# A gated two-layer Flamingo block on one core: nine barrier-ended stages merged into three regions, the local feed-forward begun inside the local attention's last steps, and one gelu moved ahead of norms

## The chip, the cores and the metric

One core of a Trainium2 chip runs the whole program. Its engines are PE (matrix multiply; PEld is its weight load), DVE (vector), ACT (activation functions), POOL (general purpose) and SP, which here only issues DMAs. The metric is the device time of one execution in microseconds (us); shorter is better. One execution was also taken by the hardware profiler; its trace is what is read below.

## The reference, cut to what matters

Four sub-blocks, each with a residual gate `tanh(g)`, on x of shape 4 x 512 x 128, all in float32 except the last.

```python
x = x + tanh(g_xattn[0]) * L0_xattn(layernorm(x), ctx)      # 16 heads over 77 keys, then layernorm, gelu FFN 128-512-128, layernorm
x = x + tanh(g_ffn[0])   * L0_ffn(layernorm(x))             # two layers, below
x = x + tanh(g_xattn[1]) * L1_xattn(layernorm(x), ctx, fside)  # 8 heads, scores gated by fside
x = x + tanh(g_ffn[1])   * L1_ffn(layernorm(x))             # one 128 x 128 product with fp8 rounding

def layer(x):                       # L0_ffn, DEPTH = 2
    q, k, v = split(shift_token(x) @ wqkv)          # 8 heads of 64
    q, k = rotary(l2norm(q) * qs, l2norm(k) * ks)
    x = x + local_attention(q, k, v) @ wo           # windows of 64, each sees itself and the one before
    h = layernorm(shift_token(x))                   # shift_token delays half of the columns by one token
    a, g = split(h @ w1 + b1)
    return x + (a * gelu(g)) @ w2 + b2
```

## The kernel before, in words

The 2048 tokens are 16 tiles of 128 (n or m = 0 to 15), four to a batch element u. x, y and base hold one row of 128 numbers per token and stay in SBUF throughout. Everything is written out by hand for each engine: an engine runs its own list in order and waits on semaphores.

There are nine stages: input and first queries; attention A (16 heads over the context); AF, the feed-forward behind it; local attention and local feed-forward of layer 0; the same two of layer 1; attention C; and the fp8 product. Each is a `stage(...)` block, which allocates its semaphores, lets each engine run its list, and ends in a barrier of all engines (L180), a clear of the stage's semaphores by POOL and a second barrier (L183).

```python
with nc.Block() as block:
    yield block, sems
nums = [s.num for s in sems]
nc.all_engine_barrier(sems_to_clear=range(min(nums), max(nums) + 1))
```

AF (L611 to L771) works per batch element u: statistics on DVE (`dve_stats`, L193 to L203), a reciprocal root on POOL (`pool_rstd`, L209), norms shared by DVE (L220) and ACT (L217), transposes on PE (L701), four hidden products (L709) with gelu on ACT (L754), `project(u)` on PE (L717, 32 matmuls), `add_ffn(u)` on DVE (L632), a second norm with the residual, `add_x(u)` (L640, L645), and a third norm that writes y, the input of layer 0. ACT's list ends in gelu(2), norm(0, y), gelu(3), norm(1, y), norm(2, y), norm(3, y).

Local attention (L789 to L1107) is a software pipeline over n = 0 to 21. At its start PE transposes y (L812), ACT copies the transposes into ht (L971, L972), and the first products are keys (L821), queries (L824) and values (L940). DVE forms the rotary products (L1030, L1033). In the last steps only the rear of the pipeline runs. For tile m these are: `values(m)` on PE (L865, L866) at step m + 4; division on DVE into `on` (L1080, L1084), called on(m) below; transposes of `on` on PE (L931) and their copy on ACT (L1011) at step m + 5; the output projection r(m) on PE (L893) and the residual addition y(m) on DVE (L1056) at step m + 6. values(m) waits for y(m - 2), since both use the same PSUM bank.

Local feed-forward (L1109 to L1266) works per u: PE shifts half the columns by one token with two matmuls (L1154, L1156), DVE takes statistics (L195, L196, L200, L203), POOL the root (L209), DVE and ACT write the two halves of the norm (L220, L217), PE transposes (L1125), ACT copies (L1183), PE makes three pairs of gate and value products (L1135, L1137), ACT the gelu (L1192), DVE the product with the value (L1240), and PE projects (L1148). `finish(u)` on DVE (L1247) adds the result to `base`, which POOL has made from y and a bias row (L1215).

Attention C (L1270 to L1478) starts with `entry(u)` on DVE (L1293), which adds the gated y to x. The last stage (L1480 on) ends in four output DMAs.

## Time and profile before

| what | us |
|---|---|
| median of the runs, lowest to highest | 763.54 (762.81 to 764.01) |
| the profiled execution's own time | 767.54 |
| its span from first to last instruction | 765.8 |
| PE busy | 592.9 (77%) |
| DVE busy | 503.5 (66%) |
| POOL busy | 418.2 (55%) |
| ACT busy | 345.0 (45%) |

Shares are means over stages with different limits. A timeline row gives the start, the duration, engine, line and operation, output and inputs, and in brackets the engine's idle time before it with what ended it. PEclk is the share of the full clock that TensorE was granted: 1.00 is 2.4 GHz and 0.50 is 1.2 GHz.

### The profile page before, as it was taken

What the parts mean: (1) busy time and instruction counts of PE and PEld (TensorE: products, weight loads), DVE (VectorE), ACT (ScalarE), POOL (GpSimd) and SP (SyncE); (2) the same over time, 40 slices, a digit from 0 to 9 for tenths busy, and PEclk for the clock granted to TensorE, in tenths of its full rate; (3) what the DMA queues carried; (4) which work ended last, traced back from release to release, by engine and by line L of the source; (5) the groups of instructions that cost most, each with busy time, mean ns of one, the idle gap of its engine ahead of it and who ended that gap; (6) DMA issues with size and microseconds to landing.
All of it is one profiled execution on the core that took longest, in us unless ns stands there. A gap on an engine that the chain in (4) does not pass through costs nothing. (4 is left out here: it accounts for less than half of the span.)

```text
span 765.8 us, 13331 instructions
## 1 busy us (share of the span) xinstructions
PE 592.9 (77%) x4922; PEld 419.2 (55%) x4922; DVE 503.5 (66%) x1117; ACT 345.0 (45%) x603; POOL 418.2 (55%) x345
## 2 busy tenths in 40 slices
PE   5679999595287999997598799999867945768701
PEld 3337777564244677776355367777753623555500
DVE  2766888636558888874543788888636336676496
ACT  2334545271156656654443566566516223343221
POOL 4545673362269999980401999999404015554320
PEclk9558999988689999999899999999998967788755
DMA  8500000000011111110000111111000000000001
GB/s 267 152 1 2 1 1 1 1 1 0 1 28 37 36 30 30 43 23 1 2 1 0 43 35 38 30 30 43 10 1 1 0 1 0 1 0 1 0 1 55
DMA packets 16142, 18.16 MB, mean 24 GB/s; under 512 B 4261, under 2 KB 10831, under 8 KB 16079
## 3 DMA queue, kind: packets, MB, share of 16 engines
q1 hardware_dynamic: 14639, 14.70, 7.5%
q10 hardware_dynamic: 1440, 2.61, 1.0%
q8 instruction: 40, 0.66, 0.4%
q14 instruction: 23, 0.19, 0.1%
HBM read 8.01 MB, written 1.05 MB: 12 GB/s over the span
## 5 line engine op out<-in xcount | busy, mean ns | idle before, releaser
L209 POOL TENSOR_TENSOR rstd<-rstd,minus_half 128x4 f32<-128x4 f32 x32 | 34.0, 1062 | 145.1 <-DVE rstd L203 145.1
L1102 POOL TENSOR_TENSOR rn<-n,minus_half 128x16 f32<-128x16 f32 x32 | 93.7, 2929 | 2.7
L1098 POOL TENSOR_TENSOR qk<-qk 128x512 f32<-128x512 f32 x64 | 80.1, 1273 | 10.8 <-DVE qk L1033 10.8
L1030 DVE TENSOR_TENSOR qk<-ps,rt 128x512 f32<-128x512 f32 x64 | 44.0, 688 | 49.1 <-ACT sq L985 33.4
L1004 ACT ACTIVATE ptb<-ps 128x512 f32<-128x512 f32 x64 | 34.7, 595 | 73.6 <-PE ps L858 73.6
L1107 POOL TENSOR_TENSOR qk<-qk,rn 128x512 f32<-128x512 f32 x64 | 65.4, 1043 | 2.5
L589 POOL TENSOR_TENSOR xy<-xy,rd 128x616 f32<-128x616 f32 x32 | 38.9, 1216 | 42.3 <-DVE rd L465 42.3
L985 ACT ACTIVATE sq<-ps 128x512 f32<-128x512 f32 x64 | 37.6, 598 | 21.9 <-PE ps L821 8.1
L546 PE MATMUL ps<-pt,vbd_a 128*128 128x128 f32 x320 | 41.7, 288 | 6.5 <-ACT pt L560 6.5
L546 PEld LDWEIGHTS ps<-pt,vbd_a 128*128 128x128 f32 x320 | 39.0, 200 | 13.5 <-issue 12.6
L1366 POOL TENSOR_TENSOR sh_c<-gt_c,mx 128x616 f32<-128x616 f32 x16 | 19.9, 1242 | 45.5 <-DVE mx L1328 45.5
L828 PEld LDWEIGHTS ps<-consts,qk 128*128 128x128 f32 x256 | 29.2, 140 | 27.4 <-issue 15.6
L1033 DVE TENSOR_TENSOR qk<-ps,rt 128x512 f32<-128x512 f32 x64 | 43.6, 681 | 0.0
L1240 DVE SCALAR_TENSOR_TENSOR qk<-ps,cols_b,pb 128x512 f32<-128x512 f32 (+1 forms) x24 | 17.8, 749 | 37.6 <-PE ps L1137 27.7
L1067 DVE TENSOR_REDUCE mx<-ps 128x8 f32<-128x1024 f32 x32 | 39.0, 1218 | 4.4 <-PE ps L852 4.4
L828 PE MATMUL ps<-consts,qk 128*128 128x128 f32 x256 | 35.3, 276 | 7.8 <-POOL qk L1107 5.4
L1071 DVE TENSOR_TENSOR pb<-ps,mx 128x1024 f32<-128x1024 f32 x32 | 39.2, 1225 | 3.0
L865 PE MATMUL ps<-vv,ptb 128*64 128x65 f32 x512 | 36.5, 224 | 4.6 <-DVE xy L1056 4.6
L893 PE MATMUL ps<-wo_b,ont 128*128 128x128 f32 x256 | 34.6, 278 | 7.0 <-ACT ont L1011 7.0
L1060 DVE TENSOR_REDUCE n<-sq 128x16 f32<-128x1024 f32 x32 | 38.7, 1209 | 0.0
L978 ACT ACTIVATE qkt<-ps 128x512 f32<-128x512 f32 x64 | 35.5, 598 | 6.8 <-PE ps L828 6.8
L850 PE MATMUL ps<-qkt 64*64 64x128 f32 x512 | 36.0, 280 | 2.8 <-ACT qkt L978 2.8
(200 smaller groups left out, 1634.6 us busy)
## 6 DMA issues: line engine op xcount, KB each, us to landing
vv<-vv SPq DMA_DIRECT2D x62, 130.0 KB, 2.3
wqkv<-in_wqkv SPq DMA_DIRECT2D x1, 1536.0 KB, 16.5
x<-in_x SPq DMA_DIRECT2D x4, 256.0 KB, 8.7
out<-xy SPq DMA_DIRECT2D x4, 256.0 KB, 2.3
w_b<-in_w_b SPq DMA_DIRECT2D x1, 682.0 KB
tmat<-in_tmat SPq DMA_DIRECT2D x1, 616.0 KB, 7.7
w<-in_w ACTq DMA_DIRECT2D x1, 512.0 KB, 4.1
rot<-in_c_rot ACTq DMA_DIRECT2D x1, 512.0 KB, 8.3
```

Of the source, the lines that this page charges most:

```text
L546: mm = pe.matmul(bank[7][:, 0:P], vbd_a[:, c, m // TPB, :], pt[:, m % 2, c, :], start=(c == 0), stop=(c == CA - 1))
L589: pool.tensor_tensor(probs(m, h), probs(m, h), rd[:, m % 2, HH * h:HH * (h + 1)].unsqueeze(2).broadcast_to([P, HH, SK]), ALU.mult).then_in ...
L828: t = pe.transpose(dst[:, c * P:(c + 1) * P], qk[:, m % 3, kind, c * P:(c + 1) * P], ident)
L985: act.activation(sq[:, kind, :], src, ACT.Square).then_inc(done, 1)
L1030: dve.tensor_tensor(qk[:, n % 3, kind].rearrange("p (h d) -> p h d", d=DH), src.rearrange("p (h d) -> p h d", d=DH), rt[:, layer, j, i:i + ...
L1033: return dve.tensor_tensor(qk2[:, kind].rearrange("p (h a e) -> p h a e", a=2, e=DH // 2), src.rearrange("p (h a e) -> p h a e", a=2, e=DH ...
L1060: dve.tensor_reduce(n2[:, n % 2, :], sq[:].rearrange("p k (h d) -> p (k h) d", d=DH), AX.X, ALU.add).then_inc(n2_done, 1)
L1067: v.do(dve.tensor_reduce(mx[:, k, 0:HB], s8, AX.X, ALU.max))
L1071: dve.tensor_tensor(pb[:, k], s8, mx[:, k, 0:HB].unsqueeze(2).broadcast_to([P, HB, P]), ALU.subtract).then_inc(s_used, 1)
L1098: pool.tensor_tensor(w, w, qk2[:, kind], ALU.add).then_inc(done, 1)
L1102: pool.tensor_tensor(rn[:, k, :], n2[:, k, :], minus_half[:], ALU.pow).then_inc(rn_done, 1)
L1107: pool.tensor_tensor(w, w, rn[:, k, HB * kind:HB * (kind + 1)].unsqueeze(2).broadcast_to([P, HB, DH]), ALU.mult).then_inc(done, 1)
```

## The change

`region()` takes over the barrier and the clear; `stage()` only adds its semaphores to the region that is open. Region one holds input and attention A, region two AF, both layers and attention C, region three the fp8 stage. So six of the eight inner stage ends are gone, and waits on data take their place. Each layer's attention and feed-forward are now one stage. PE's `flip` of y is called `turn`, each turn waits for its own u, and the fourth stands behind the first step's products. The feed-forward's shifts, statistics, norms and first transposes stand at the ends of steps 18 (NT + LS), 19 (NT + LP) and 20 (NT + LV) of the attention, in other PSUM banks than before. In AF, gelu(3) stands ahead of norm(0, y). The tiles of attention C are views of `vv`, and three memsets are made for layer 0 only. The diff, cut, without the changes of indentation:

```diff
-        def stage(*names):
+        def region():
             with ExitStack() as c:
-                sems = [c.enter_context(nc.semaphore(n)) for n in names]
+                sems = []
                 with nc.Block() as block:
-                    yield block, sems
+                    open_regions.append((block, c, sems))
+                    yield
+                    open_regions.pop()
                 nums = [s.num for s in sems]
                 nc.all_engine_barrier(sems_to_clear=range(min(nums), max(nums) + 1))
+        def stage(*names):
+            block, c, sems = open_regions[-1]
+            mine = [c.enter_context(nc.semaphore(f"{n}_{len(sems)}")) for n in names]
+            sems.extend(mine)
+            yield block, mine
...
@@ attention A, PE, ahead of score(0, 0) @@
+                            pe.wait_ge(vbd_done, CA + CC)
+                            pe.wait_ge(kbd_done, U)
+                            pe.wait_ge(q_done, U)
@@ attention A, ACT, ahead of the first exp; POOL, ahead of its first memset and of the gates @@
+                                        if n == 0 and h == 0:
+                                            act.wait_ge(query_done, U)
+                            pool.wait_ge(query_done, U)
+                            pool.wait_ge(tg_done, 1)
...
@@ AF, ACT @@
                         gelu(2)
-                    norm(0, y, x, nmr3)
                         gelu(3)
-                    norm(1, y, x, nmr3)
+                        norm(0, y, x, nmr3, yn_act)
+                        norm(1, y, x, nmr3, yn_act)
...
@@ local attention, PE @@
+                            def turn(u):
+                                if layer == 0:
+                                    pe.wait_ge(yn_dve, 2 * (u + 1))
+                                    pe.wait_ge(yn_act, 2 * (u + 1))
+                                else:
+                                    pe.wait_ge(y_ready, u + 1)
...
-                        for u in range(U):
-                            flip(u)
+                            turn(0)
+                            turn(1)
+                            turn(2)
                             keys(0)
                             queries(0)
                             for n in range(NT + LR):
...
+                                if n == 0:
+                                    turn(3)
+                                if n == NT + LS:
+                                    pe.wait_ge(qt_done, NT)
+                                    shift_in(0)
+                                    shift_in(1).then_inc(sh_raw, 1)
+                                if n == NT + LP:
+                                    pe.wait_ge(s_used, NT)
+                                    shift_in(2).then_inc(sh_raw, 1)
+                                if n == NT + LV:
+                                    pe.wait_ge(lffn_in, LFFN_IN)
+                                    flip(0)
+                                    flip(1)
+                            hidden(0)
+                            shift_in(3).then_inc(sh_raw, 1)
+                            flip(2)
+                            hidden(1)
...
@@ local attention, ACT, at a step's end @@
+                                if n == NT + LP:
+                                    norm(0)
+                                if n == NT + LV:
+                                    act.wait_ge(lffn_in, LFFN_IN)
+                                    norm(1)
+                                    flipped(0)
+                            flipped(1)
+                            norm(2)
+                            gelu(0)
+                            flipped(2)
+                            gelu(1)
+                            norm(3)
+                            flipped(3)
...
@@ local attention, DVE, at a step's end @@
+                                if n == NT + LS:
+                                    stats(0)
+                                if n == NT + LP:
+                                    norm(0)
+                                    stats(1)
+                                if n == NT + LV:
+                                    norm(1)
+                                    stats(2)
+                            dve.wait_ge(lffn_in, LFFN_IN)
+                            norm(2)
+                            hidden(0)
+                            stats(3)
+                            hidden(1)
+                            norm(3)
+                            hidden(2)
...
@@ POOL, behind the attention's last step; biased(u) makes the base sums @@
+                            pool_rstd(pool, 0, var_ready, rstd_ready)
+                            pool_rstd(pool, 1, var_ready, rstd_ready)
+                            biased(0)
+                            pool_rstd(pool, 2, var_ready, rstd_ready)
+                            biased(1)
+                            biased(2)
+                            pool_rstd(pool, 3, var_ready, rstd_ready)
+                            biased(3)
...
@@ attention C, DVE @@
                         def entry(u):
+                            dve.wait_ge(y_done, u + 1)
```

ACT's list at the end of AF, of the kernel before (L754 is the gelu, L217 a norm, two rows' worth per batch element, L746 the copy of the transposes, L971 the first copy of layer 0):

```order
L754 ACTIVATE hidt<-ps,cols 128x512 x4
L746 ACTIVATE xt<-ps,cols 128x512
L754 ACTIVATE hidt<-ps,cols 128x512 x4
L217 ACTIVATE xy<-x,nmr,rstd 128x128 x2
L754 ACTIVATE hidt<-ps,cols 128x512 x4
L217 ACTIVATE xy<-x,nmr,rstd 128x128 x6
L180 UNCONDITIONAL_BRANCH
L967 UNCONDITIONAL_BRANCH
L971 ACTIVATE ht<-ps 64x512
```

and of the change (the gelu is now L778, the norm L230, the copies L770 and L1085):

```order
L778 ACTIVATE hidt<-ps,cols 128x512 x4
L770 ACTIVATE xt<-ps,cols 128x512
L778 ACTIVATE hidt<-ps,cols 128x512 x8
L230 ACTIVATE xy<-x,nmr,rstd 128x128 x8
L1081 UNCONDITIONAL_BRANCH
L1085 ACTIVATE ht<-ps 64x512
```

The last four gelus stand directly behind the four before them, and all eight norms of y behind those.

PE's list at the end of layer 0's attention, of the kernel before, from the last output transposes on (L931 transposes of `on`, L893 output projection, L1154 and L1156 shifts, L1125 transposes of the norm, L1135 and L1137 gate and value products):

```order
L931 MATMUL ps<-consts,on 128x128 x4
L893 MATMUL ps<-wo_b,ont 128x128 x4
L931 MATMUL ps<-consts,on 128x128 x4
L893 MATMUL ps<-wo_b,ont 128x128 x4
L180 UNCONDITIONAL_BRANCH
L1117 UNCONDITIONAL_BRANCH
L1154 MATMUL ps<-xy,consts 128x256
L1156 MATMUL ps<-xy,consts 128x192
```

and of the change (L1021 transposes of `on`, L953 and L955 shifts, L983 output projection, L918 transposes of the norm, L933 and L935 gate and value products):

```order
L1021 MATMUL ps<-consts,on 128x128 x4
L953 MATMUL ps<-xy,consts 128x256
L955 MATMUL ps<-xy,consts 128x192
L983 MATMUL ps<-wo_b,ont 128x128 x4
L1021 MATMUL ps<-consts,on 128x128 x4
L918 MATMUL ps<-consts,xy 128x128 x8
L983 MATMUL ps<-wo_b,ont 128x128 x4
L933 MATMUL ps<-xt,w_b 128x512
L935 MATMUL ps<-xt,w_b 128x512
```

The transposes flip(0) and flip(1) (L918, eight) stand ahead of the last output projection, and the third batch element's shift between the transposes of tiles 14 and 15.

DVE's list at the same place, of the change (L1232 the residual addition y(m), L1256 and L1260 the division, L226 and L233 bias and norm, L208 on the statistics):

```order
L1256 RECIPROCAL rd<-ps 128x8 [waits o_raw_21]
L1260 TENSOR_TENSOR on<-ps,rd 128x512 [waits ont_raw_21,v_chain_21]
L226 SCALAR_TENSOR_TENSOR nmr<-mv,rstd 128x4 [waits rstd_ready_21]
L233 TENSOR_SCALAR xy<-ps,mv,rstd 128x64 x4
L208 BN_STATS st<-xy 128x6 [waits sh_raw_21]
```

The norm of u = 0 and the statistics of u = 1 stand between on(15) and the addition y(14), where nothing stood before.

## Rows read from the trace of the kernel before

**Rows 1.** Timeline at the first stage end (start us, us, engine, line, operation)
```profile
41.81 0.20 ACT L304 ACTIVATE tg<-vecs 128x4 f32<-128x4 f32 x1
...
42.85 0.46 PE L502 MATMUL ps<-mrow_bf,ones_bf 1*128 1x308 bf16 x4 [1.65 <-PEq L183]
```

**Rows 2.** POOL's semaphore clears (line L183): count, duration ns min/median/max, first and last start
```profile
L183 POOLq EVENT_SEMAPHORE_RANGE_CLEAR  x9: 111/219/761, 42.5 to 765.0; - x9
```

**Rows 3.** Timeline of AF's second half
```profile
177.97 3.73 PE L717 MATMUL ps<-wa,hidt 128*128 128x128 f32 x32
...
187.79 0.88 ACT L217 ACTIVATE xy<-x,nmr,rstd 128x128 f32<-128x128 f32 x2 [15.94 <-DVE nmr L213]
...
191.03 5.57 PE L717 MATMUL ps<-wa,hidt 128*128 128x128 f32 x32 [9.32 <-ACT hidt L754]
...
196.63 0.69 DVE L632 TENSOR_TENSOR base<-ps,base 128x512 f32<-128x512 f32 x1 [8.36 <-PE ps L717]
```

**Rows 4.** Timeline of layer 0, attention's end and feed-forward's front
```profile
357.07 0.69 DVE L1084 TENSOR_TENSOR on<-ps,rd 128x512 f32<-128x512 f32 x1 [1.32 <-PE ps L931]
...
359.03 0.29 DVE L1056 TENSOR_TENSOR xy<-ps,xy 128x128 f32<-128x128 f32 x1 [1.27 <-PE ps L893]
...
361.42 0.69 DVE L1084 TENSOR_TENSOR on<-ps,rd 128x512 f32<-128x512 f32 x1 [0.45 <-PE ps L931]
...
363.82 0.60 ACT L1011 ACTIVATE ont<-ps 128x512 f32<-128x512 f32 x1 [1.87 <-PE ps L931]
...
365.66 0.29 DVE L1056 TENSOR_TENSOR xy<-ps,xy 128x128 f32<-128x128 f32 x1 [1.99 <-PE ps L893]
...
367.25 0.67 PE L1154 MATMUL ps<-xy,consts 128*128 128x256 f32 x2 [1.63 <-PEq L183]
...
369.11 0.23 DVE L195 BATCH_NORM_STATS2 st<-xy 128x6 f32<-128x64 f32 x1 [3.16 <-PE ps L1156]
...
370.98 1.01 POOL L209 TENSOR_TENSOR rstd<-rstd,minus_half 128x4 f32<-128x4 f32 x1 [28.51 <-DVE rstd L203]
...
372.58 1.09 DVE L220 TENSOR_SCALAR xy<-ps,mv,rstd 128x64 f32<-128x64 f32 x4
...
372.76 1.43 ACT L217 ACTIVATE xy<-xy,nmr,rstd 128x64 f32<-128x64 f32 x4 [8.35 <-DVE nmr L213]
...
374.34 0.63 PE L1125 MATMUL ps<-consts,xy 128*128 128x128 f32 x4 [3.83 <-ACT xy L217]
...
380.29 1.28 ACT L1192 ACT_TABLE_LOAD   x1
...
381.59 0.69 ACT L1192 ACTIVATE pb<-ps,cols_b 128x512 f32<-128x512 f32 x1
```

**Rows 5.** Timeline of layer 1's attention end, first gelu, and attention C's first step
```profile
568.34 0.29 DVE L1056 TENSOR_TENSOR xy<-ps,xy 128x128 f32<-128x128 f32 x1 [1.99 <-PE ps L893]
...
583.87 0.69 ACT L1192 ACTIVATE pb<-ps,cols_b 128x512 f32<-128x512 f32 x1
...
617.47 0.75 DVE L1293 SCALAR_TENSOR_TENSOR x<-xy,tg,x 128x512 f32<-128x512 f32 x1 [1.44 <-PEq L183]
```

**Rows 6.** Timeline of layer 0's start
```profile
211.13 0.59 ACT L971 ACTIVATE ht<-ps 64x512 f32<-64x512 f32 x1 [1.92 <-PE ps L812]
...
213.44 1.89 PE L821 MATMUL ps<-wqkv,ht 128*128 128x512 f32 x2
...
216.00 0.69 DVE L1030 TENSOR_TENSOR qk<-ps,rt 128x512 f32<-128x512 f32 x1 [7.18 <-ACT sq L985]
```

**Rows 7.** Windows of 3 us: busy by engine, PEclk (granted share), DMA, GB/s
```profile
186.00:189.00 3.00, 0.00 (x0) 0.00 (x0) 2.17 (x13) 1.21 (x3) 1.11 (x1) 0.50 0.00 0
...
376.00:379.00 3.00, 1.95 (x6) 1.46 (x7) 2.93 (x20) 2.40 (x6) 1.23 (x2) 0.50 0.00 0
...
397.00:400.00 3.00, 3.00 (x8) 1.19 (x7) 1.28 (x2) 1.34 (x2) 0.00 (x0) 1.00 0.03 5
```

**Rows 8.** Timeline of layer 1's start, DVE
```profile
418.61 0.69 DVE L1030 TENSOR_TENSOR qk<-ps,rt 128x512 f32<-128x512 f32 x1 [4.53 <-ACT sq L985]
```

More of the change, by code:

```diff
@@ L325, in _ @@
-                        pe.wait_ge(kt_done, 1)
-                        for k in range(CC):
-                            o, h0 = P * k % SK, chunk_head(k, HC)
-                            w = WIN * DC
-                            mm = pe.matmul((bank[6], bank[7], bank[0])[k // 2][:, U * w * (k % 2):U * w * (k % 2 + 1)],
-                                           sel[0:SK, o:o + P], vraw[0:SK, :, 1, h0 * DC:h0 * DC + w], start=True, stop=True)
-                            if k != 0 and k != 2:
-                                mm.then_inc(vc_raw, 1)
@@ L333, in _, with flip @@
-                        pe.wait_ge(kt_done, 2)
-                        for u in range(U):
+                        def flip(u):
                             pe.wait_ge(xn_dve, 2 * (u + 1))
@@ L1175, in _, with norm @@
                     def _(act):
-                        def norm(u):
+                        def norm(u, dst, src, nmr_ready, done=None):
                             act.wait_ge(nmr_ready, u + 1)
-                            for n in range(TPB * u, TPB * (u + 1)):
-                                act_norm(act, n, xn[:, n, 0:64], y[:, n, 0:64]).then_inc(xn_act, 1)
+                            for n in (TPB * u + 2, TPB * u + 3):
+                                ins = act_norm(act, n, dst[:, n, :], src[:, n, :])
+                                if done is not None:
+                                    ins.then_inc(done, 1)
@@ L1195, in _ @@
-                        act.wait_ge(lffn_in, LFFN_IN)
-                        norm(0)
-                        norm(1)
+                            for c in range(NC):
+                                act.wait_ge(h_raw, NC * u + c + 1)
+                                if u >= 2:
+                                    act.wait_ge(f_raw, u - 1)
+                                act.activation(hidt[:, u % 2, c, :], bank[2 + c], ACT.Gelu, bias=b1_a[:, c:c + 1]).then_inc(h_done, 1)
+                        norm(0, xn, base, nmr1, xn_act)
@@ L1198, in _ @@
+                        norm(1, xn, base, nmr1, xn_act)
                         flipped(0)
                         flipped(1)
-                        norm(2)
+                        norm(2, xn, base, nmr1, xn_act)
                         gelu(0)
-                        norm(3)
+                        norm(3, xn, base, nmr1, xn_act)
                         flipped(2)
@@ new lines, in _ @@
+                            pe.wait_ge(xq_done, u + 1)
+                            for j in range(TPB):
+                                t = pe.transpose(bank[u].bitcast(BF16)[:, j * P:(j + 1) * P], xq[:, TPB * u + j, :], ident_bf[:])
+                            t.then_inc(xqt_raw, 1)
+                            pe.wait_ge(xqt_done, u + 1)
+                            for j in range(TPB):
+                                mm = pe.matmul(bank[4 + u][:, j * P:(j + 1) * P], xqt[:, u, j * P:(j + 1) * P], kern_q[:],
+                                               start=True, stop=True)
@@ L1253, in _ @@
                         norm(0)
-                        stats(2)
                         norm(1)
-                        stats(3)
                         norm(2)
-                        hidden(0)
+                        project(0)
                         norm(3)
-                        hidden(1)
-                        hidden(2)
-                        finish(0)
-                        hidden(3)
-                        finish(1)
-                        finish(2)
-                        finish(3)
@@ L1586, in flamingo_kernel, with _ @@
+                        project(1)
+                        project(2)
+                        project(3)
+                    @block.sync
+                    def _(sp):
+                        dst = out.rearrange("(u j p) d -> u p j d", p=P, u=U)
+                        for u in range(U):
+                            sp.wait_ge(y_done, u + 1)
+                            sp.dma_start(dst[u], y[:, sl(u), :]).then_inc(stored, 16)
+                        sp.wait_ge(stored, 16 * U)
         nums = [s.num for s in held]
```

2275 lines of the change are left out of this document (1123 added, 1152 removed).

## The prediction

> **What bounds the kernel now.** I read the page first, then the order of work at each stage end, then the clock. Over the whole span no engine is the limit: PE, the busiest, is busy 77%. So the question is which wait ends last in each stretch that the change touches, and I followed the chain there.
>
> The kernel has nine stages, and at each stage end the reader sees an emptying and refilling. At the first, ACT's last operation ends at 42.01 and the first matmul of the next stage starts at 42.85 [rows 1]: 0.84 us in which nothing computes. That is one barrier's own price. POOL clears the stage's semaphores there, 0.11 to 0.76 us, nine times [rows 2].
>
> The second thing to see is in the AF feed-forward. project(2) is on PE from 177.97 for 3.73 us, so project(3) could follow at 181.7, but it starts at 191.03 after 9.32 us of idle "<-ACT hidt" [rows 3]. ACT had idled 15.94 us before 187.79, because its queue holds norm(0, y) ahead of gelu(3), and that norm waits for a DVE/POOL chain of another batch element [rows 3]. Then DVE idles 8.36 us until project(3) is done, at 196.63 [rows 3].
>
> The third is the local feed-forward's front. From the attention's last residual add y(15) at 365.66 to the first gelu at 381.59 are 15.9 us [rows 4] in which PE has little to do: shifts, statistics, reciprocal roots, norms, transposes, one table load. Layer 1 repeats it, 568.34 to 583.87 [rows 5].
>
> **Part 1: AF's gelu(3) ahead of its norms.** hidden(3) precedes project(2) on PE, so gelu(3)'s inputs are there before 178.0, and ACT is free from 187.79 - 15.94 = 171.85. gelu(3) is done by about 178.8, and project(3) runs at 181.7 to 185.4, in full-clock time (3.73). It is then no longer the limit. What is late next is DVE, which still has add_x(1) and norm(0): it reaches add_ffn(3) at about 188.25 (ACT's norm(0), released by the same chain, starts at 187.79 today). So add_ffn(3) moves from 196.63 to 188.25, **8.4 us**, and everything behind it (a DVE/POOL chain without PE) moves along. norm(0, y) on ACT is not delayed: gelu(3) is over nine us before it.
>
> **Part 2: no barrier between AF and layer 0.** Today DVE idles 7.18 us before the first product at 216.00 [rows 6]. Afterwards the turns 0 to 2 run as norms arrive. ACT's last norm ended at 211.13 - 1.92 = 209.2 [rows 6], so now at 200.8; two copies of 0.59 [rows 6] give 202.0; keys(0) takes 1.89 at the half clock that PE has there [rows 6], and from its end to the product are 0.67 (216.00 - 213.44 - 1.89). That is 204.7 instead of 216.0, 11.3 in all and 2.9 beyond part 1. But today sixteen transposes warm PE before keys(0); now they are spread out, so queries(0) also runs slow, which takes back some 0.5. Ends: 1.9 (the third matmul slow too) and 3.8 (full clock, keys in 1.0). I take **2.7**, near the slow end, since the clock row says 0.50 after a similar silence [rows 7].
>
> **Part 3: the feed-forward begins inside the attention's last steps**, layer 0 on the old clock. shift_in(0) and (1) stand behind the transposes that release on(14) at 357.07. They take 1.86 (367.25 to the first statistics at 369.11), the statistics 1.87 (to POOL at 370.98) [rows 4]. DVE serves in order, so y(13) goes from 359.03 to about 360.7. values(15) waits for y(13), so the 2.39 from there to on(15) (361.42 - 359.03) shift whole, to 363.1. Behind on(15) (0.69) come norm(0), about 1.2 with its bias, and stats(1), 1.87: 366.9. POOL's root takes 1.01, ACT's norm(1) 1.43 [rows 4]: 369.5. PE meanwhile holds flip(1) ahead of the last output projection r(15), so r(15) is **queued behind a wait that is not its own**: flip 0.63, then 1.24 for r(15) (363.82 + 0.60 to 365.66), and y(15) falls at 371.4, 5.7 later than today. stats(2) fits beside that, ending near 371.0; root 1.01, norm(2) 1.43, table load 1.28 [rows 4] bring the first gelu to 374.85 instead of 381.59: 6.7 earlier. In layer 1 the same front is 0.4 shorter today (15.5), so 6.3.
>
> From there to the end of the feed-forward PE sets the pace, and I find no lost ground: shift_in(3) adds under 1 us on PE between hidden(0) and flip(2), and stats(3) 1.87 on DVE, but norm(3) with its 1.43 on ACT leaves that place, and now stands beside gelu and project work. POOL's four base sums run while POOL would idle; their waits for r_done queue only rstd(2) and rstd(3), whose inputs come later. SP's copies keep their order.
>
> The clock decides how much of 13.0 stays. PE would idle from about 366 to 369.5, and stands at 0.50 in 376 to 379 today after such a lull [rows 7]. If the gate falls here, the second and third gate/value pairs of hidden(0) are late by 0 to 1.7 per layer. Nearest is today's first front, which also ran at half and lost little, as ACT's table load covers the first pair. I take 0.6 each: 13.0 - 1.2 = **11.8**. Ends: 9.6 and 13.0, and, if the hand schedule of the tail is wrong by 1 us a layer, 14.
>
> **Part 4: the remaining stage ends.** Input to attention A: 0.84 goes nearly whole, as the scores wait for the last query copy instead: **0.8** (0.6 to 0.85). Layer 0 to layer 1: DVE idles 4.53 before 418.61 [rows 8], so its last finish ended at 414.08. Without the barrier turn(0) runs beside that finish, right behind project(3) (done about 414.0), four copies of 0.59 end at 416.4, square 0.6: 417.0, so **1.6** (1.2 to 1.7). Layer 1 to attention C: DVE idles 1.44 on the barrier [rows 5]; its next operation reads its own last result, so **1.4** go. Three memsets of POOL vanish in layer 1, hidden anyway. Against it: the two clears that stay inside handle 45 and some 140 semaphores instead of 16 and 26. The rows [rows 2] don't grow evenly, so I bound this by 0 and 1.3 and take **0.7** lost.
>
> **Sum.** 8.4 + 2.7 + 11.8 + 0.8 + 1.6 + 1.4 - 0.7 = 26.0 us. The profiled execution took 767.54, so 741.5 for one like it; it lies 4.0 above the median of the runs, 763.54. Against that median: **737.5 us**. With all low ends (8.0 + 1.9 + 9.6 + 0.6 + 1.2 + 1.3 - 1.3 = 21.3) it is 742.2, with all high ones (8.5 + 3.8 + 14 + 0.85 + 1.7 + 1.45) 733.2.
>
> **Rivals.**
> - *PE stays warm* (0.16): the spread-out transposes keep the clock up. Then part 2 gives 3.8 and part 3 its 13.0: 735 to 734. For it: PE's pauses in the tail are shorter than the nine us of AF's. Against it: 0.50 at 376 to 379, after less [rows 7].
> - *The overlap eats itself* (0.10): the attention's tail is a chain through all engines, and r(15) behind flip(1), values(15) behind y(13) behind stats(0) delay it as much as the front advances. Then part 3 is worth only what a barrier is, about 1.3 each (365.95 to 367.25): 26.0 - 11.8 + 2.6 = 16.8, 746.7. For it: my 5.7 us of delay. Against it: the front itself needs 15.9.
> - *AF's chain does not move* (0.05): norm(0, y) or a POOL root holds add_ffn(3): 763.5 - 17.6 = 745.9.
> - *It does not do what it says* (0.03): the new waits fall due where the barriers stood, since the scores of stage two wait for everything. Without part 4's 3.8: 741.3.
> - *Slower: the feed-forwards run at half clock* (0.02). Project(3) shows the price: 5.57 us begun at half clock, against project(2)'s 3.73 [rows 3]. PE sets the pace from first gelu to last finish, 32.5 us a layer. If the activity left in the tail never lifts the gate, both stretches double at most: up to 737.5 + 65 = 802.5. It decides from 26 us of added time on, 13 a layer; today the low stretch around 376 to 379 costs the PE-bound part little. The Trainium skill, page "TensorE: Matmul & The Clock Gate", Part 1, "What's actually happening", says the default state is throttled and activity releases the throttle; by that rule alone the thinned-out tail could start each feed-forward cold. The trace agrees that the clock falls in lulls, but shows it back at 1.00 in the dense stretch from 397 to 400 [rows 7], which is why the chance is small.
>
> **How the numbers follow.** The forecast (parts at their taken values, 735 to 742.5) has 0.64. The range 732 to 746 takes in the warm case, the hand schedule's error, the misplaced AF chain and the missing part 4; it leaves out the eaten overlap and half clock, and some of the forecast's own tail. About 0.2% (1.5 us) is what a measurement of this kernel tells from no change. No case but the slow one comes near it: faster 0.97, same 0.01, slower 0.02.
>
> **What would show it.** In the changed profile: project(3) straight after project(2), add_ffn(3) some 8.4 earlier, no 9 us idle on PE; the first product of layer 0 about 4 us after ACT's last norm; in each tail y(13) about 1.7 and y(15) about 5.7 late, PE waiting some 3.5 us before flip(1), and the first gelu 3 to 4 us after y(15) instead of 15.9; first-gelu-to-finish unchanged at 32.5; 0.1 us between DVE's last finish and attention C. Wrong if y(15) moves by over 8 us, if first-gelu-to-finish grows by over 2, or if the clock is at 0.50 in the middle of a feed-forward.

## The result and the profile after

The changed kernel takes **737.28 us** (median of four executions, 735.30 to 737.69) against 763.77 for the kernel before (762.81 to 765.05): ratio 0.965, 95% interval 0.962 to 0.968. Measured again as the yardstick of the first experiments it was 737.71 against 764.61, ratio 0.966 (0.962 to 0.970). The forecast was 737.5. The profiled execution took 737.42, span 735.6.

A timeline row reads as in the rows ahead of the prediction. First AF and layer 0's entry, changed kernel, rows of PE, ACT and DVE.

```profile
176.53 7.31 PE L741 MATMUL ps<-wa,hidt 128*128 128x128 f32 x64
...
176.73 0.69 ACT L778 ACTIVATE hidt<-ps,cols 128x512 f32<-128x512 f32 x1 [0.17 <-PE ps L733]
...
186.75 0.69 DVE L656 TENSOR_TENSOR base<-ps,base 128x512 f32<-128x512 f32 x1
...
198.45 0.88 ACT L230 ACTIVATE xy<-x,nmr,rstd 128x128 f32<-128x128 f32 x2 [0.44 <-DVE nmr L226]
...
200.47 2.07 PE L865 MATMUL ps<-wqkv,ht 128*128 128x512 f32 x2 [1.23 <-ACT ht L1086]
...
203.21 0.69 DVE L1178 TENSOR_TENSOR qk<-ps,rt 128x512 f32<-128x512 f32 x1 [4.03 <-ACT sq L1099]
```

project(2) and project(3) are one row now, 64 matmuls in 7.31 us, since the last gelu (176.73) is done before project(2) is half over. The nine idle us of PE [rows 3] are gone, and DVE's add_ffn(3) follows its own earlier work without a wait. From project(2)'s start to add_ffn(3) it took 196.63 - 177.97 = 18.66 us and now takes 186.75 - 176.53 = 10.22: **8.44** gained. From ACT's last norm to the first product it was 216.00 - 209.21 = 6.79 [rows 6] and is 203.21 - 199.33 = 3.88.

Layer 0's tail, changed kernel, timelines of PE, of DVE, of POOL and of ACT.

```profile
358.03 0.63 PE L918 MATMUL ps<-consts,xy 128*128 128x128 f32 x4 [4.33 <-DVE xy L233]
358.49 1.87 PE L983 MATMUL ps<-wo_b,ont 128*128 128x128 f32 x8
360.16 1.92 PE L933 MATMUL ps<-xt,w_b 128*128 128x512 f32 x2
```

```profile
345.06 0.69 DVE L1260 TENSOR_TENSOR on<-ps,rd 128x512 f32<-128x512 f32 x1 [1.32 <-PE ps L1021]
...
348.21 0.28 DVE L1232 TENSOR_TENSOR xy<-ps,xy 128x128 f32<-128x128 f32 x1
...
355.19 1.22 DVE L226 SCALAR_TENSOR_TENSOR nmr<-mv,rstd 128x4 f32<-128x4 f32 x1 [0.93 <-POOL rstd L222]
...
360.40 0.29 DVE L1232 TENSOR_TENSOR xy<-ps,xy 128x128 f32<-128x128 f32 x1 [1.29 <-PE ps L983]
360.61 0.85 DVE L226 SCALAR_TENSOR_TENSOR nmr<-mv,rstd 128x4 f32<-128x4 f32 x1
```

```profile
355.12 1.26 POOL L1309 TENSOR_TENSOR base<-xy,row_b 128x512 f32<-128x512 f32 x1
359.19 1.02 POOL L222 TENSOR_TENSOR rstd<-rstd,minus_half 128x4 f32<-128x4 f32 x1 [2.81 <-DVE rstd L216]
360.18 2.49 POOL L1309 TENSOR_TENSOR base<-xy,row_b 128x512 f32<-128x512 f32 x2
```

```profile
362.95 1.28 ACT L1117 ACT_TABLE_LOAD   x1
364.25 1.27 ACT L1117 ACTIVATE pb<-ps,cols_b 128x512 f32<-128x512 f32 x2
```

PE waits 4.33 us ahead of flip(1) with r(15) queued behind it, so y(15) is added at 360.40. Counted from on(14), which is 357.07 before [rows 4] and 345.06 now, y(15) is 15.34 - 8.59 = 6.75 us later than it was, y(13) 3.15 - 1.96 = 1.19 later, and the first gelu 24.52 - 19.19 = 5.33 earlier. The gelu now comes 3.85 us behind y(15), against 15.93. Windows of that stretch; the last three columns are the granted clock, the DMA share and GB/s.

```profile
353.00:356.00 3.00, 0.63 (x4) 0.42 (x4) 2.00 (x11) 0.58 (x1) 1.86 (x2) 1.00 0.00 0
356.00:359.00 3.00, 0.97 (x7) 1.00 (x8) 2.93 (x18) 2.41 (x6) 0.38 (x1) 0.92 0.00 0
359.00:362.00 3.00, 3.00 (x10) 1.97 (x10) 1.71 (x6) 0.97 (x3) 2.81 (x3) 0.51 0.00 0
362.00:365.00 3.00, 2.65 (x7) 0.86 (x5) 0.48 (x2) 2.97 (x6) 0.67 (x1) 1.00 0.00 0
```

After the lull the clock is at half for some 3 us, which r(15) (1.87 us for eight matmuls) and the first gate products (1.92) pay; then it is full. The remaining stage ends of the changed kernel follow. First PE's timeline at attention A's first score:

```profile
42.40 0.46 PE L516 MATMUL ps<-mrow_bf,ones_bf 1*128 1x308 bf16 x4 [0.87 <-ACT qt L316]
```

PE idles 0.87 us there, against 1.65 [rows 1]: 0.78 gained. Then DVE's timeline, and the two ACT and DVE rows of layer 1 that answer to [rows 5].

```profile
395.64 0.69 DVE L1212 TENSOR_TENSOR xy<-ps,base 128x512 f32<-128x512 f32 x1 [1.99 <-PE ps L946]
399.15 0.69 DVE L1178 TENSOR_TENSOR qk<-ps,rt 128x512 f32<-128x512 f32 x1 [2.82 <-ACT sq L1099]
...
556.12 0.29 DVE L1232 TENSOR_TENSOR xy<-ps,xy 128x128 f32<-128x128 f32 x1 [1.75 <-PE ps L983]
...
559.51 1.27 ACT L1117 ACTIVATE pb<-ps,cols_b 128x512 f32<-128x512 f32 x2
...
590.91 0.69 DVE L1212 TENSOR_TENSOR xy<-ps,base 128x512 f32<-128x512 f32 x1 [1.99 <-PE ps L946]
591.52 0.74 DVE L1350 SCALAR_TENSOR_TENSOR x<-xy,tg,x 128x512 f32<-128x512 f32 x1
```

Layer 1's first product comes 2.82 us behind the last finish, against 4.53 [rows 8], and attention C's entry follows the last finish directly. From layer 1's first product to the end of its last finish it was 616.03 - 418.61 = 197.42 and is 591.60 - 399.15 = 192.45, so **5.0** gained in layer 1 (4.97). The clears left in the changed kernel, count and least, median and greatest duration in ns:

```profile
L188 POOLq EVENT_SEMAPHORE_RANGE_CLEAR  x3: 108/287/822, 145.1 to 735.0; - x3
```

287 ns stand at the end of attention A, where 112 stood, and 822 at the end of attention C, where 259 stood.

### The profile page after: what moved, and what is told of

It is laid out like the page before. It is cut to its first block and busy times, and to the rows that moved or that the text cites. A ratio compares the mean times of both kernels' runs of the same rounds, so it can differ in the third digit from the quotient of the medians.

```text
span 735.6 us, 13205 instructions
## 1 busy us (share of the span) xinstructions
PE 584.8 (79%) x4922; PEld 412.7 (56%) x4922; DVE 506.6 (69%) x1117; ACT 346.6 (47%) x603; POOL 417.7 (57%) x342
## 5 line engine op out<-in xcount | busy, mean ns | idle before, releaser
L1137 ACT ACTIVATE ptb<-ps 128x512 f32<-128x512 f32 x64 | 34.8, 595 | 72.5 <-PE ps L902 72.5
L1423 POOL TENSOR_TENSOR vv<-vv,mx 128x616 f32<-128x616 f32 x16 | 19.9, 1243 | 44.5 <-DVE mx L1385 44.5
L563 PE MATMUL ps<-pt,vbd_a 128*128 128x128 f32 x320 | 39.5, 279 | 6.8 <-ACT pt L577 6.8
L563 PEld LDWEIGHTS ps<-pt,vbd_a 128*128 128x128 f32 x320 | 36.9, 192 | 13.4 <-issue 12.9
L1236 DVE TENSOR_REDUCE n<-sq 128x16 f32<-128x1024 f32 x32 | 38.7, 1209 | 0.0
L909 PEld LDWEIGHTS ps<-vv,ptb 128*64 128x64 f32 x512 | 32.2, 137 | 10.7 <-issue 10.7
```

The lines of the kernel that those rows point to most:

```text
L563: mm = pe.matmul(bank[7][:, 0:P], vbd_a[:, c, m // TPB, :], pt[:, m % 2, c, :], start=(c == 0), stop=(c == CA - 1))
L909: pe.matmul(o[0:64], ptb[:, i, 0:64], vv[:, m % RING, 1, h, :], start=True, stop=True)
L1236: dve.tensor_reduce(n2[:, n % 2, :], sq[:].rearrange("p k (h d) -> p (k h) d", d=DH), AX.X, ALU.add).then_inc(n2_done, 1)
```

## The experiments

Medians are of six executions of each kernel (four for x5) and ratios are to the kernel before, measured beside it. Runs x1 to x4 shared one chip, x5 to x8 a second, x9 to x12 a third; on them the kernel before took 764.61, 764.61 and 763.94. A median set against x1 or x6 below is therefore in part one of another chip. Single executions of one kernel lie up to 10 us apart, so gains of one or two us are read from stretches of the traces, and the medians stand beside them. "The tail" below is the time from y(12) of a layer to the start of its last finish: 59.59 (layer 0) and 58.95 (layer 1) before, 53.86 and 53.94 after.

**x1, the changed kernel again.** No edit.

> The changed kernel itself, nothing edited, as the yardstick for the three edits that follow it on the same chip. All theories: 737.3 us as before, with single executions between 735 and 738. Between two traces of the same code, single stretches of attention A and C may differ by up to 4 us, if it is right that their clock phases and not the change made the profiled pair differ by 30.1 us where the medians differ by 26.5.

Measured: 737.71 (736.21 to 741.05). In its trace, stage one and attention A up to the end took 143.30, against 144.28 in the first trace, but divided otherwise: 38.45 to the first score and 104.84 from there to the last add, against 42.40 and 101.88. From AF on each stretch repeats to 0.2 us. So stretches of identical code do differ by 3 to 4 us, as expected.

**x2, the gelu put back.**

```diff
-                        gelu(3)
                         norm(0, y, x, nmr3, yn_act)
+                        gelu(3)
```

> The changed kernel with AF's fourth gelu put back behind its norms, everything else as changed. Theory (the 8.4 us are the head-of-line wait of gelu(3), which delays turn and project(3) and all behind them): 745.7 us, that is 8.4 us above the changed kernel, and the DVE add behind AF's last project comes about 8.4 us later than 186.75. Rival (the removed barrier behind AF, not the order of two instructions, lets the end of AF move; put back, the gelu costs little as layer 0 can begin beside it): 738 to 741 us.

Measured: 746.57, ratio 0.976 (0.972 to 0.980), 8.9 above x1. PE and ACT timelines of x2:

```profile
188.00 6.11 PE L741 MATMUL ps<-wa,hidt 128*128 128x128 f32 x32 [9.32 <-ACT hidt L778]
```

```profile
184.77 0.88 ACT L230 ACTIVATE xy<-x,nmr,rstd 128x128 f32<-128x128 f32 x2 [15.94 <-DVE nmr L226]
```

The 15.94 and the 9.32 of [rows 3] are back to the hundredth, with no barrier near. From add_ffn(2) to add_ffn(3) it is 15.42 against 6.45. The theory holds; the rival is out.

**x5, the same edit in the kernel before, alone.**

```diff
-                    norm(0, y, x, nmr3)
                     gelu(3)
+                    norm(0, y, x, nmr3)
```

> The kernel before with one edit: AF's fourth gelu stands ahead of its last norms, all barriers kept. Theory (two instructions in the wrong order, nothing else, make the 8.4 us): 755.4 us, 8.4 below the kernel before, and the mirror of putting it back in the changed kernel (which cost 8.9). Rival (the gain needs the missing barrier too): 760 us or more.

Measured: 755.15, ratio 0.987 (0.980 to 0.994). From add_ffn(2) to add_ffn(3) it is 6.45 against 14.89. Eight us come from the order of two instructions, with the barriers or without.

**x3, the front behind the attention.** The same edit on PE, ACT and DVE:

```diff
-                                if n == NT + LS:
-                                    pe.wait_ge(qt_done, NT)
-                                    shift_in(0)
...
+                            pe.wait_ge(qt_done, NT)
+                            pe.wait_ge(r_done, NT)
+                            shift_in(0)
+                            shift_in(1).then_inc(sh_raw, 1)
+                            pe.wait_ge(s_used, NT)
+                            shift_in(2).then_inc(sh_raw, 1)
+                            pe.wait_ge(lffn_in, LFFN_IN)
+                            flip(0)
+                            flip(1)
```

> The changed kernel with the feed-forward's shifts, statistics, first two norms and flips taken out of the attention loop and put directly behind it, in both layers; no barrier comes back. Theory (the overlap with the last attention steps is worth what the trace shows, 5.7 us in layer 0 and 5.0 us in layer 1, of which the barriers and clears that stay removed give 2.4 us together): 745.6 us; y(15) is added some 6 us earlier in both layers than the changed kernel has it (360.40), and the first gelu some 4 us later (364.25). Rival (the overlap eats itself: what it wins in front it loses again as the attention's last two steps wait behind the flips, and only the missing barrier counts): 737 to 739 us.

Measured: 748.68, ratio 0.979 (0.976 to 0.983), 11.0 above x1. The tails are 59.19 and 59.20, 10.6 us longer in the two layers together, nearly as long as before, though no barrier stands in them. The overlap is worth more than expected, and the missing barrier alone nothing: the first shift does come earlier behind y(15) (0.39 us against 1.59), but DVE loses that again. DVE's and POOL's timeline of x3:

```profile
360.42 0.16 DVE L226 SCALAR_TENSOR_TENSOR nmr<-mv,rstd 128x4 f32<-128x4 f32 x1
...
361.63 1.22 DVE L226 SCALAR_TENSOR_TENSOR nmr<-mv,rstd 128x4 f32<-128x4 f32 x1
...
366.76 1.15 DVE L226 SCALAR_TENSOR_TENSOR nmr<-mv,rstd 128x4 f32<-128x4 f32 x1 [1.20 <-POOL rstd L222]
```

```profile
361.56 1.26 POOL L1302 TENSOR_TENSOR base<-xy,row_b 128x512 f32<-128x512 f32 x1
```

The operation that makes nmr takes 0.16 us when POOL is idle. The second starts 0.07 us behind a POOL addition and ends 0.03 us behind it. The two slow ones lose 2.1 us a layer here, and 1.8 and 1.3 in the changed kernel, so about 1 of the 10.6 us is a longer stall and not the missing overlap. This pointed at x6.

**x4, the second flip behind r(15).**

```diff
-                                    flip(1)
+                            flip(1)
```

> The changed kernel with only the second flip of the feed-forward taken out of the attention loop, so that it stands behind r(15) on PE and r(15) no longer waits 4.3 us behind it. Theory (the first gelu hangs on the third norm, which hangs on statistics that DVE takes in the same order anyway; y(15) only just binds): y(15) about 1.2 us earlier, first gelu 0.4 us earlier in each layer, 736.5 us. Rival (the 6.7 us delay of y(15) is on the path and its 4.3 us come back in each layer): 729 us.

Measured: 737.50 (737.15 to 741.14), ratio 0.966 (0.963 to 0.970): no change against x1. y(15) stands 17.30 behind y(12) instead of 18.61, so 1.3 earlier, and the tails are as long as before the edit (53.92 and 53.84). So y(15) can come 1.3 us earlier without anything behind it doing so, and the 729 us of the rival are out. The expected 0.4 did not appear either: nmr(2) starts 0.23 earlier but ends where POOL's addition ends. This shows that r(15)'s wait behind the second flip costs nothing beside that addition, not that it is off the path without it (see x6).

**x6, POOL's additions ahead of its powers.**

```diff
                             pool.wait_ge(lffn_in, LFFN_IN)
+                            biased(0)
+                            biased(1)
+                            biased(2)
                             pool_rstd(pool, 0, var_ready, rstd_ready)
                             pool_rstd(pool, 1, var_ready, rstd_ready)
-                            biased(0)
                             pool_rstd(pool, 2, var_ready, rstd_ready)
-                            biased(1)
-                            biased(2)
                             pool_rstd(pool, 3, var_ready, rstd_ready)
```

> The changed kernel with POOL's first three additions of the feed-forward's bias moved ahead of its four powers, into POOL's idle time before 348 us. Theory (the short DVE operation that makes nmr(1) and nmr(2) takes 1.21 and 0.86 us instead of 0.15 because it stands still until POOL's addition, which began 0.1 us ahead of it or earlier, has ended; both lie on the chain to the first gelu): nmr back at 0.15 us, y(15) 1.06 us and the first gelu 1.5 to 1.7 us earlier in each layer, 734.5 us. Rival (nmr is slow for another reason, or its wait is covered by the wait of r(15)): 737.3 to 737.7 us.

Measured: 732.50 (731.70 to 734.61), ratio 0.959 (0.955 to 0.964). DVE's and PE's timelines of x6, layer 0:

```profile
353.29 0.16 DVE L226 SCALAR_TENSOR_TENSOR nmr<-mv,rstd 128x4 f32<-128x4 f32 x1 [0.93 <-POOL rstd L222]
...
357.36 0.16 DVE L226 SCALAR_TENSOR_TENSOR nmr<-mv,rstd 128x4 f32<-128x4 f32 x1 [0.42 <-POOL rstd L222]
```

```profile
355.08 0.63 PE L918 MATMUL ps<-consts,xy 128*128 128x128 f32 x4 [3.27 <-DVE xy L233]
355.55 1.06 PE L983 MATMUL ps<-wo_b,ont 128*128 128x128 f32 x8
```

nmr is back at 0.16 us, and the tails are 51.79 and 52.55: 2.1 and 1.4 us shorter, about what was expected. A bonus in layer 0 is that PE's lull is 3.27 instead of 4.33 us and the clock does not fall, so r(15) takes 1.06 us. In layer 1 it fell all the same, and there DVE's timeline shows y(15) directly ahead of nmr(2), with no wait for POOL:

```profile
551.01 0.29 DVE L1232 TENSOR_TENSOR xy<-ps,xy 128x128 f32<-128x128 f32 x1 [1.75 <-PE ps L983]
551.22 0.15 DVE L226 SCALAR_TENSOR_TENSOR nmr<-mv,rstd 128x4 f32<-128x4 f32 x1
```

POOL's root was done at 550.36. So without the additions the late y(15) is on the path in layer 1 and holds nmr(2) up by about 0.8 us; what x4 found holds only beside them. The median moved by 5.2, of which these traces account for 3.5; the rest is open. The Trainium skill, page "SBUF — State Buffer", section "Who interferes with whom", says that a DVE instruction with two inputs in SBUF contends with a GpSimd instruction that reads SBUF, and that the ports they share are an exclusive lock. nmr and POOL's addition are such a pair, and these rows agree (1.22 us beside 0.16).

**x7, PE kept busy between the flips.** `warm(k, b)` issues k matmuls of 128x512, with weights from wqkv, into a bank b that nobody reads.

```diff
                                     flip(0)
+                                    warm(4, bank[1])
                                     flip(1)
```

> The changed kernel with four more matmuls of 128x512 into a bank that nobody reads, between the two flips in the attention loop, where PE stood idle for 4.3 us; the result is not touched. Clock theory (r(15) and the first products of the feed-forward run at half clock, since PE did nothing for 4.3 us before them): r(15) 1.1 us in place of 1.9, no product of 1.9 us behind it, y(15) and the first gelu 0.7 us earlier in layer 0 and 0.5 us in layer 1, 736.3 us. Rival (the half clock is hidden, the first gelu hangs on POOL and DVE): 737.3 to 737.7 us. If the four matmuls hold up the second flip, slower by up to 1 us.

Measured: 741.88 (738.95 to 744.40), ratio 0.971 (0.966 to 0.976): 4.2 slower than x1 by the medians, whose executions overlap, and 3.0 by the two tails. The matmuls did what they were meant to: r(15) takes 1.06 us, and y(15) stands 0.8 us nearer to y(12). But the first gelu does not come earlier (22.46 behind y(12) in both), since POOL's addition holds nmr(2) as before, and PE now finishes its first two pairs of products early and waits there. Windows and PE's timeline of x7:

```profile
359.00:362.00 3.00, 2.17 (x6) 0.63 (x4) 1.67 (x5) 2.29 (x5) 1.86 (x2) 1.00 0.00 0
362.00:365.00 3.00, 0.96 (x2) 0.37 (x3) 1.41 (x2) 1.69 (x3) 0.00 (x0) 0.75 0.00 0
365.00:368.00 3.00, 3.00 (x9) 1.50 (x8) 0.57 (x1) 0.68 (x1) 0.00 (x0) 0.68 0.00 0
```

```profile
364.04 2.00 PE L933 MATMUL ps<-xt,w_b 128*85 128x512 f32 x2 [2.87 <-DVE qk L1210]
```

The half clock moved from r(15), where it is hidden behind POOL's addition, to the third pair of products, where it is not: the tails are 55.25 and 55.53, 1.4 and 1.6 us longer. The rival was right that the cost is hidden; that it would come back elsewhere neither theory had.

**x8, PE kept busy at layer 0's start.**

```diff
+                            warm(4, bank[5])
                             turn(0)
+                            warm(6, bank[5])
                             turn(1)
+                            warm(3, bank[5])
                             turn(2)
+                            warm(1, bank[5])
                             keys(0)
```

> The changed kernel with 14 more matmuls of 128x512 into a bank that nobody reads, where PE waits between AF's last project and layer 0's first keys; the result is not touched. Clock theory (layer 0's first keys, queries and values take 1.9 us at half clock instead of 1.1, and the first product waits for them; the prediction took 0.5 us off for that): the first product and what follows 1.3 to 1.8 us earlier, 736 us. Rival (the entry hangs on ACT's copies, not on PE): 737.3 to 737.7 us.

Measured: 737.37 (733.31 to 738.17), ratio 0.964 (0.960 to 0.969). PE's timeline of x8:

```profile
203.60 1.13 PE L865 MATMUL ps<-wqkv,ht 128*128 128x512 f32 x2 [0.83 <-ACT ht L1098]
204.57 1.02 PE L868 MATMUL ps<-wqkv,ht 128*128 128x512 f32 x2
```

Keys and queries take 1.1 us instead of 2, and from add_ffn(3) to the first step's reduction (L1236) it is 17.94 instead of 19.36 us: 1.4 gained, as expected. The first product itself comes only 0.9 earlier (15.54 instead of 16.46), less than the 1.3 to 1.8 expected. The median gained 0.3, which is too little to tell from none.

**x9, the gelu table loaded early.** As x6, with one unread element ahead of the second norm:

```diff
                                     act.wait_ge(lffn_in, LFFN_IN)
+                                    act.activation(gel[0:1, 1, 0:1], cols_b[0:1, layer, 5:6], ACT.Gelu)
                                     norm(1)
```

> The kernel with POOL's additions ahead (732.5 us), and on ACT one gelu of a single element, which nothing reads, ahead of the feed-forward's second norm, where ACT idles for 1.9 us. Theory (the load of the gelu table, 1.28 us between the third norm and the first gelu, lies on the chain and is taken in that idle time): first gelu 1.28 us earlier in each layer, 2.6 us in all, 729.9 us. Rival (the copies and norms behind the small gelu bring another table back, so that a second load follows): 732.5 us or 1 to 3 us more.

Measured: 731.46 (728.58 to 737.70), ratio 0.959 (0.954 to 0.964). ACT's timeline of x9, layer 0:

```profile
356.98 1.28 ACT L1160 ACT_TABLE_LOAD   x1
358.27 0.20 ACT L1160 ACTIVATE pb<-cols_b 1x1 f32<-1x1 f32 x1
358.76 1.43 ACT L230 ACTIVATE xy<-xy,nmr,rstd 128x64 f32<-128x64 f32 x4 [0.28 <-DVE nmr L226]
...
364.85 0.67 ACT L1117 ACTIVATE pb<-ps,cols_b 128x512 f32<-128x512 f32 x1
```

The load stands in idle time, and norms, copies and gelus follow without another, so the rival is out. The theory is borne out in layer 1, where the first gelu comes 1.5 us earlier behind y(12) than in x6 and the tail is 1.5 us shorter. In layer 0 the gelu comes 0.7 earlier, but the clock was at 0.50 from 359 to 365 in this execution, and the tail is 0.6 longer. The median lies 1.0 below x6's and 1.6 above the 729.9 expected; with executions 9 us apart it decides nothing.

**x10, the first gelus ahead of the third norm.** x6 and x4's edit, and:

```diff
                             flipped(1)
-                            norm(2)
                             gelu(0)
+                            norm(2)
```

> The kernel with POOL's additions ahead (732.5 us), the second flip behind r(15) on PE, and on ACT the first group's gelus ahead of the third norm. Theory (the first gelu does not need the third norm, only the first two flips; the table load then stands beside DVE's part of that norm): first gelu 2 to 2.5 us earlier in each layer and the third flip 2.5 us earlier, 727.5 us. Rival (the third norm is what all later work hangs on, and it only moves behind three gelus): 732 us or slower.

Measured: 729.92 (729.20 to 731.35), ratio 0.957 (0.953 to 0.961). The first gelu comes 2.5 and 3.1 us earlier behind y(12) than in x6, as expected or more. The tails are 50.05 and 50.14: 1.7 and 2.4 us shorter than in x6, so not all of it lasts to the end, and the median fell by 2.6 where 5.0 was expected. No run has x4's edit with x6's alone; as y(15) was on the path in x6's layer 1, up to 0.8 us of that layer's gain can be due to x4's edit and not to the gelus' place.

**x11, x9's and x10's edits together.**

> The two edits of the runs before together: the gelu of one element ahead of the second norm, and the first group's gelus ahead of the third norm. Theory: the first gelu 3.4 us earlier in each layer than with POOL's additions alone, the third flip 2.9 us earlier, 726.5 us. Rival (the two take the same time away, DVE's multiplications behind the norm are the bound): as without the early load, 727.5 us.

Measured: 731.09 (729.10 to 733.67), ratio 0.959 (0.954 to 0.963). The tails are 49.86 and 49.84, 0.2 and 0.3 shorter than in x10, so the two edits take the same time away. ACT's timeline of x11, layer 1, shows the next bound:

```profile
552.91 0.69 ACT L1117 ACTIVATE pb<-ps,cols_b 128x512 f32<-128x512 f32 x1 [0.34 <-PE ps L933]
554.63 0.69 ACT L1117 ACTIVATE pb<-ps,cols_b 128x512 f32<-128x512 f32 x1 [1.03 <-PE ps L933]
556.47 0.68 ACT L1117 ACTIVATE pb<-ps,cols_b 85x512 f32<-85x512 f32 x1 [1.16 <-PE ps L933]
```

Each gelu waits for PE, which makes the products behind the second flip almost without a pause. The rival was right that nothing is gained over x10 (its 727.5 us, like the theory's 726.5, was too low), and wrong in naming DVE.

**x12, x11 with x8's matmuls.**

> The run before, and the 14 unread matmuls of 128x512 at layer 0's start. Theory (they gave 1.6 us in the trace of the run that had them alone, though the medians did not show it): 725 us. Rival: no difference, 726.5 us.

Measured: **727.28** (726.13 to 730.16), ratio 0.954 (0.949 to 0.958), 1.4% below the changed kernel's 737.71 and faster than both kernels. Layer 0's start is 1.4 us shorter, its tail 1.3 longer (half clock there in this execution), layer 1 the same. So the two stretches that the matmuls touch or may touch cancel to 0.1 us in this trace. The median fell by 3.8 against x11, more than the 1.5 expected. The two profiled executions differ by 3.5, and attention A, which the matmuls do not touch, took 101.91 in this trace and 104.98 in that of x11. Whether the matmuls gain anything is open.

## Why the prediction was right, point by point

| term | predicted | measured in the traces |
|---|---|---|
| 1: gelu(3) ahead of its norms | 8.4 | 8.44; put back +8.9, alone 9.5 by medians |
| 2: no barrier from AF to layer 0 | 2.7 | 2.91 - 0.51 = 2.40 |
| 3: front inside the attention's tail | 11.8 | 5.74 + 4.97 = 10.7 |
| 4: input to A, 0 to 1, 1 to C | 0.8, 1.6, 1.4 | 0.78, 1.71, 1.52 |
| 4: larger clears | -0.7 | -0.18 - 0.56 = -0.74 |
| sum | 26.0 | 24.8 |

The 0.51 of term 2 is what the first step loses behind its first product, where keys, queries and values run at half clock (2.07 and 1.91 us); 0.5 was taken off for it. Term 3 in layer 0 is 5.33 up to the first gelu and 0.41 from there to the end.

Against 24.8 the medians moved by 26.5 and 26.9, and the profiled pair by 30.1. Most of the pair's excess lies in code that the change does not touch. From first score to first add, attention A took 20.2 in the trace of before and 17.3 in that of after, and attention C's 16 adds took 78.59 and 74.61. In x5, which keeps every barrier, those adds took 74.49, so the 4.0 us there are not the change's. The trace of before was a slow one in this stretch, as its time, 4 us above its median, already said. Two stretches run the other way. From attention A's last add to AF's third it is 34.42 us before and 36.02 after, but 35.91 in x5, so most of that is not the change's either. And attention A's adds 2 to 16 take 84.62 us where they took 84.29; all runs of the changed kernel have 84.61 to 84.64 and x5 has 84.32, so these 0.3 us are a loss by the change that no term holds. Its cause is open. The 1.7 to 2.1 us by which the medians exceed the sum are within such shifts and are not assigned. Taken from the median of 763.54, the 24.8 us of the terms give 738.7; that the result came within 0.2 us of the forecast is luck to that extent. The 1.5 us that the prediction took for the noise fit the medians of the kernel before (763.5 to 764.6), but not its single executions, which lie between 759.0 and 768.8.

**The term that was mis-sized** is part 3: 13.0 - 1.2 = 11.8 predicted, 10.7 measured. Its error is the net of two misses. Up to the first gelu, 6.7 and 6.3 us were to be gained; counted from on(14) it was 5.33 in layer 0 and, with (583.87 - 559.75) - (559.51 - 540.33), 4.94 in layer 1. Behind the first gelu 0.6 a layer was taken off for the half clock, and nothing was lost there (0.41 and 0.08 gained). The half clock came, but in layer 0 the first gate products, which it slowed, ended at 362.08, and the table load ahead of the first gelu only at 364.23.

The sentence that fails is "POOL's four base sums run while POOL would idle". POOL does idle there, but its additions stop DVE: nmr(1) took 1.22 us and nmr(2) 0.85 (0.40 in layer 1) where the kernel before has 0.15, on the chain to the first gelu. Moved away, they gave 3.5 us back (x6). y(15) was reckoned 5.7 us late and came 6.75 late: flip(1) began 12.97 us behind on(14) where 12.43 were reckoned, with nmr(1) ahead of it, and from flip(1) to y(15) it took 2.37 instead of 1.87, as r(15) ran at half clock. The step asked who waits for POOL, and not what POOL's work does to DVE. The trace of the kernel before had the answer, where attention C begins (POOL's and DVE's timelines):

```profile
620.82 1.26 POOL L1354 TENSOR_TENSOR base<-x,gated_rows 128x512 f32<-128x512 f32 x1
```

```profile
620.88 1.22 DVE L213 SCALAR_TENSOR_TENSOR nmr<-mv,rstd 128x4 f32<-128x4 f32 x1 [1.13 <-POOL rstd L209]
```

The same operation, begun 0.06 us behind an addition of POOL, ended 0.02 us behind it.

**The rivals.** *PE stays warm* did not come: the clock was at 0.50 at layer 0's start, at 0.51 in its tail, and at 0.68 and 0.75 in the two windows from 552 to 558 in layer 1's. Its price for part 2, 3.8 us, is confirmed by x8: from add_ffn(3) to the first product it was 216.00 - 196.63 = 19.37 before and is 15.54 there. *The overlap eats itself*: the delay it spoke of is there, but x4 shows that r(15)'s part of it costs nothing beside POOL's addition, and x3 that the overlap brings nearly all of term 3. *AF's chain does not move* falls with x2 and x5, *it does not do what it says* with the 0.78, 1.71 and 1.52. *The feed-forwards run at half clock*: from first gelu to last finish it is 31.39 against 31.80. By the rule of the Trainium skill, page "TensorE: Matmul & The Clock Gate", Part 1, "What's actually happening", that the clock is throttled until activity releases it, the thinner tail starts colder. The trace agrees for some 3 us per layer, and shows 1.00 in the window from 362 on.

**What was to be seen.** The predicted 3.5 us wait before flip(1) was 4.33, the first gelu came 3.85 and 3.39 behind y(15) (3 to 4 predicted), and y(13) was 1.19 late (1.7 predicted). Each layer's feed-forward kept its length (32.09 from first gelu to the end of the last finish, 32.5 predicted), and attention C's entry follows the last finish at once. The errors of the terms are all within 1.1 us.

## What to carry to other kernels

Before removing barriers, look for an instruction whose engine holds it behind another chain's wait: here two swapped lines of one queue gave 8.4 of some 26 us. When work of two engines is laid side by side, ask of each short DVE operation on the chain which POOL operation now runs beside it, for one that reads two SBUF tensors may stand still until POOL's is over, as nmr did here. And before warming PE in a lull, ask what PE waits for behind it: in x7 the half clock left work that hid it and landed on work that did not. An edit that gains nothing may also be masked by another wait of the same length, as x4 was by POOL's addition.

## What was not expected of the hardware

Identical code meets the rising clock at different times. In attention A the clock was still 0.50 at 57 to 60 us in one execution (x4) and 1.00 in another of the same code there (the changed kernel), with the stage begun at 42.67 and 42.40. Windows of x4, then of the changed kernel:

```profile
57.00:60.00 3.00, 3.00 (x16) 3.00 (x15) 1.52 (x3) 0.26 (x1) 2.39 (x2) 0.50 0.00 0
```

```profile
57.00:60.00 3.00, 3.00 (x27) 2.46 (x26) 1.58 (x4) 0.37 (x1) 2.26 (x2) 1.00 0.00 0
```

The stage takes 104.8 us in the one and 101.9 in the other. The shift of 3 to 4 us in attention A, and likewise in the first stage and attention C, is larger than most single edits tried here; whoever compares one trace with one trace must leave such stretches out.

The price of a clear of semaphores does not follow their number alone. It was 0.29 us for 45 and 0.82 for 145, where 16 and 26 had taken 0.11 and 0.26. But in the kernel before, the 15 semaphores of each layer's local feed-forward took 0.11 us at the end of layer 0 (414.58) and 0.76 at the end of layer 1 (616.52). Why is open.
